# Two output instructions per image in place of four, in a convolution kernel paced by VectorE

## The reference

```python
def _gn(v, G=32, eps=1e-05):            # group norm, 4 channels a group, no affine part
    g = v.reshape(B_, G, C_ // G, H_, W_)
    m = jnp.mean(g, axis=(2, 3, 4), keepdims=True)
    s = jnp.var(g, axis=(2, 3, 4), keepdims=True)
    return ((g - m) / jnp.sqrt(s + eps)).reshape(v.shape)

wq = ternary(weight)                    # Wp, -Wn or 0 by a threshold
out = conv_general_dilated(x_, wq, (1, 1), padding=((1, 1), (1, 1)))   # 128 -> 128, 3 x 3
x = x + (out(_gn(x)) + bias[None, :, None, None])
```

## Time and profile before

| | |
|---|---|
| median of 3 runs | 581.22 us (580.83, 581.22, 588.1) |
| profiled execution | 588.38 us, span 586.6 us |
| DVE busy | 545.3 us, 93%, 508 instructions |
| PE busy | 535.1 us, 91%, 3223 matmuls |
| ACT busy | 504.4 us, 86% |
| POOL busy | 172.5 us, 29% |
| mean granted TensorE clock | 0.984 |
| moved by DMA | 153.35 MB, mean 261 GB/s |

### The profile page before, as it was taken

How to read it: one execution, slowest core, us unless ns; L and a number is a source line. 1 busy time by engine, 2 the same in 40 slices (tenths; PEclk the granted TensorE clock), 3 DMA queues, 4 the chain that set the end, 5 groups by cost and what they waited for, 6 DMA issues and landing times.

```text
span 586.6 us, 9218 instructions
## 1 busy us (share of the span) xinstructions
PE 535.1 (91%) x3223; PEld 319.1 (54%) x3223; DVE 545.3 (93%) x508; ACT 504.4 (86%) x482; POOL 172.5 (29%) x108
## 2 busy tenths in 40 slices
PE   0368999999999999999999799999999999999993
PEld 0234555555555555555565455655555555555551
DVE  2986999999999999999999879999999999999972
ACT  2478999998999999998998689999999999999840
POOL 1203222333332223333332133322233333222372
PEclk9979999999999999999999989999999999999998
DMA  7400999999999999999999998999999999999765
GB/s 289 189 0 2 287 279 284 285 276 297 296 303 272 298 282 291 283 299 290 289 289 251 269 267 264 300 289 269 285 286 281 302 296 297 292 275 270 208 152 224
DMA packets 27954, 153.35 MB, mean 261 GB/s; under 512 B 3488, under 2 KB 3488, under 8 KB 27936
## 3 DMA queue, kind: packets, MB, share of 16 engines
q1 hardware_dynamic: 19008, 103.36, 46.5%
q0 software_dynamic: 8928, 49.78, 42.0%
HBM read 51.97 MB, written 51.38 MB: 176 GB/s over the span
## 4 chain that ended last, share of the span: by engine, by line
DVE 62%; issue 23%; DMA 5%; PE 4%; POOL 2%; ACT 2%; DVEq 1%; POOLq 1%; SPq 0%; ACTq 0%
DVE parts L556 22%; DVE y L566 16%; DVE plane L514 10%; DVE plane L520 8%; PE even_rows L651 2%; DMA y<-x 2%; DMA x<-in_x_dram 2%; DVE newton L545 1%; PE odd_rows L651 1%; POOL plane L294 1%; POOL c_sb L320 1%; DVE plane L526 1%; DVEq L150 1%; DMA y<-in_L_conv_weight_dram 1%; DVE neg_var L534 1%
## 5 line engine op out<-in xcount | busy, mean ns | idle before, releaser
L651 PE MATMUL odd_rows<-parts,w_lhsT 128*128 128x385 f16 (+1 forms) x1536 | 268.9, 332 | 7.8 <-DVE parts L556 7.6
L651 PE MATMUL even_rows<-parts,w_lhsT 128*128 128x385 f16 (+1 forms) x1536 | 266.9, 331 | 9.5 <-DVE parts L556 7.0
L556 DVE SCALAR_TENSOR_TENSOR parts<-plane,norm_scale,parts 128x1568 f16<-128x1568 f32 x128 | 235.3, 1845 | 5.3 <-ACT parts L368 5.2
L294 POOL TENSOR_TENSOR plane<-x 128x1512 f32<-128x1512 f32 x32 | 109.1, 3409 | 388.1 <-DVE parts L556 379.9
L651 PEld LDWEIGHTS even_rows<-parts,w_lhsT 128*128 128x128 f16 x1536 | 149.8, 98 | 116.9 <-issue 12.6
L368 ACT ACTIVATE parts<-plane,norm_scale 128x1568 f16<-128x1568 f32 x128 | 201.2, 1597 | 11.8 <-ACT plane L389 5.3
L651 PEld LDWEIGHTS odd_rows<-parts,w_lhsT 128*128 128x128 f16 x1536 | 149.1, 100 | 109.2 <-DVE parts L556 9.6
L374 ACT ACTIVATE junk<-x 128x3136 f16<-128x3136 f32 x32 | 89.9, 2809 | 18.7 <-DMA x<-in_x_dram 18.6
L395 ACT ACTIVATE junk<-x,negmean 128x3136 f16<-128x3136 f32 x32 | 93.0, 2906 | 0.1
L566 DVE SCALAR_TENSOR_TENSOR y<-even_rows,out_scale,d_sb 128x784 f32<-128x784 f32 x64 | 63.2, 1028 | 6.3 <-POOL d_sb L320 6.3
L566 DVE SCALAR_TENSOR_TENSOR y<-odd_rows,out_scale,c_sb 128x784 f32<-128x784 f32 x64 | 63.1, 1027 | 1.6 <-PE odd_rows L651 1.6
(11 more groups left out here) (53 smaller groups left out, 107.8 us busy)
## 6 DMA issues: line engine op xcount, KB each, us to landing
x<-in_x_dram SPq DMA_DIRECT2D x64, 784.0 KB, 7.1
out_dram<-y SPq DMA_DIRECT2D x64, 784.0 KB, 5.5
y<-x POOLq DMA_DIRECT2D x62, 784.0 KB, 8.6
y<-in_L_conv_weight_dram SPq DMA_DIRECT2D x1, 576.0 KB, 3.6
bias_sb<-in_L_conv_bias_dram SPq DMA_DIRECT2D x1, 0.5 KB, 3.2
wp_sb<-in_L_conv_Wp_dram SPq DMA_DIRECT2D x1, 0.5 KB, 3.6
wn_sb<-in_L_conv_Wn_dram SPq DMA_DIRECT2D x1, 0.5 KB, 4.3
```

What stands on the lines that cost most here:

```text
L294: nc.gpsimd.tensor_tensor(plane[B][:, 0:PAIRS - 1, :], even[:, 0:PAIRS - 1, :], even[:, 1:, :], ALU.subtract).then_inc(plane_ready[B], 1)
L556: nc.vector.scalar_tensor_tensor(part(img, j, LO), plane[j][:], norm_scale[:, b_slice(img)], part(img, j, HI), ALU.mult, ALU.subtract).the ...
L651: ins = nc.tensor.matmul(product_ps(odd, b, b + 1)[:, 0, :, to:to + n], w_lhsT[:, prod, kw, :], part(img, prod, which)[:, b * BANK_ROWS:(b ...
```

## The change

For every image but the last, VectorE issues one output instruction over all four banks of the even rows, then one over those of the odd rows, 1568 columns each. Each waits for the whole product, for both halves' stores of the image two before, and adds 2 to its count when it is done. The last image keeps its four halves.

```diff
+                def output_image(img, odd):
+                    prod, other, ready, done = ((A, d_sb, d_ready, even_done), (B, c_sb, c_ready, odd_done))[odd]
+                    dve.wait_ge(product_done[prod], img.half(HALVES - 1, 1, 1))
+                    dve.wait_ge(ready, img.count(plus=1))
+                    for h in range(HALVES):
+                        wait(dve, y_stored[img.pair][h], img.pair_turns(16))
+                    y = y_sb[img.pair][:].rearrange("p (b r o) w -> p b r o w", b=BANKS, o=2)[:, :, :, odd, :]
+                    nc.vector.scalar_tensor_tensor(y, product_ps(odd), out_scale[:, p, 0:1], other[:],
+                                                   ALU.mult, ALU.add).then_inc(done, HALVES)
...
-                    if now:
+                    if now and nxt:
+                        output_image(now, EVEN)
+                        output_image(now, ODD)
+                    elif now:
                         for odd in (EVEN, ODD):
                             for h in range(HALVES):
-                                output_rows(now, h, odd, last=not nxt)
+                                output_rows(now, h, odd, last=True)
```

## The result

| | before | changed |
|---|---|---|
| median of 6 runs | 586.82 us (580.83 to 597.51) | 601.26 us (600.83 to 602.77) |
| profiled execution | 588.38 us, span 586.6 | 602.27 us, span 600.5 |
| period of a steady image | 16.62 us | 17.31 us |

The ratio is 1.0296, 95% interval 1.0253 to 1.0338: slower. It compares the fast runs alone (597.51 is left out of it, 2.9% above the fastest of its kernel), while the medians are those of all runs. The three runs of before that came with the result (597.51, 585.53, 589.23) lie above the 580.83 and 581.22 that the prediction started from; the changed kernel's six lie within 2 us.

A forecast was written before the change was run, and what follows sets the result against it. VectorE was taken to bound the kernel by its issue order. From 581.46 us, 30 periods each 0.70 longer (+ 21.0) and the last slot (+ 0.7) gave 603.2 us, +3.8%, range 599 to 609.5.

The forecast's parts named there:

- VectorE bounds, with a saving of 0.24 us per image: VectorE's issue order sets the 16.62 us period; fusing saves a fixed part of about 0.12 us per output.
- C waits for the whole even output: TensorE's next product C starts at s + 1.92 instead of s + 1.16, s being the even output's start.
- L534 and its slack of 0.07 us: VectorE's variance operation, reading a sum formed behind C, starts at s + 6.22 after idling 0.94 us.
- Period 17.32: Next even output 11.10 us after L534, so 17.32 us per steady image against 16.62: +0.70.
- the ring over two images: With L534's wait gone, the odd output's wait for all of product B gives periods of 16.5 on average.
- The covers: TensorE, ScalarE, GpSimd and DMA do not bind first; GpSimd's residual issue comes only 0.1 to 0.2 us later.
- The last slot, + 0.7: After output 30, C's late start delays ScalarE's copy and GpSimd's adds by 0.6 to 0.8 us: + 0.7.
- The kept saving (1): VectorE's 0.24 us per image come through: 574 us, or 578 with a two-image ring; decided at L534; 4%.
- the partial one (2): No measurable change, up to 592 us: ScalarE or TensorE catches up, so half the added wait disappears; 3%.
- the clock (3): TensorE's new idle of 0.9 us per image brings one slow product each, + 30 x 2.9, about 690 us; 3%.
- (4): Late loads remain as in the profiled execution and the 588.1 run: up to 610 us; 10%.
- The step that took 581.46 as the time of before: Profiled execution 588.38 less 6.92 us for three slots stretched by a late load of x: 581.46.

The follow-up runs named there:

- Experiments 1: Changed kernel with one parity fused, the other in halves: even only 602.46 us, ratio 1.0271; odd only 582.31 us, ratio 0.9965.
- experiment 2: Kernel before, nothing fused, but banks 0 and 1 of product C wait for both even halves: 607.1 us, ratio 1.0353.
- Experiment 3: Changed kernel with L534 behind the low part of A: 584.11 us; or instead with the variance matmul ahead of C's last bank: 583.04 us.
- experiments 1 to 5: Those listed here, plus controls with L534 behind A's low part: kernel before, nothing fused, 586.62 us; only odd output fused, 582.34 us.
- experiment 5: First-half loads one slot earlier, SP's list without a loop: kernel before 583.14 us; changed kernel 604.15; odd output fused with L534 moved 579.72.
- experiment 6: Changed kernel with L534 behind A's low part, earlier loads, and next image's plane A made between the two outputs: 649.37 us, ratio 1.1056.

## Why the prediction was right, step by step

- **VectorE bounds, with a saving of 0.24 us per image.** Right. Both fused outputs are 1.84 us long and 1.76 apart from what follows; with the wait away, the short one of the alternating periods is 16.37 = 16.62 - 0.25.
- **C waits for the whole even output.** Forecast s + 1.92, measured s + 1.91. Experiments 1 and 2 show that this wait is the whole loss in each period: with it alone the loss is there, without it (odd only) it isn't.
- **L534 and its slack of 0.07 us.** Forecast s + 6.22, measured s + 6.22; idle 0.94 forecast, 0.85 measured as the profile counts idle time, from the end of an instruction and not from its next start. Experiment 3 shows that this is the one path: two unlike cuts of it bring the period back.
- **Period 17.32.** Measured 17.31. The forecast of the ring over two images once this wait is gone (16.5 on average, through product B and the odd output) held too: 16.37 and 16.64 in turn. In the slot where the odd output waits for B it begins 2.02 us instead of 1.76 behind the even one, and the period that follows is the 16.64.
- **The covers.** GpSimd's residual issue came at s + 4.17, not at s + 3.6 to 3.7: it starts 0.57 us after the odd output's end, with up to 0.6 us of idle in 29 slots. I had put that latency too low. Nothing that binds stood behind it: no load came late in the loop. ScalarE's copy of C waited as said, from s + 6.1.
- **The last slot, + 0.7.** Wrong, in its sign too: the profiled execution is 1.56 us shorter behind output 30. ScalarE's copy of C did start 0.8 us later, and so did GpSimd's first add into c_sb, but counted from output 30 that add ended no later: it took 3.60 us before and 2.53 after, and ended 1.7 us behind the end of VectorE's last low part in both traces (568.07 to 569.77 before, 583.28 to 584.97 after). So VectorE's row of instructions set it, 0.25 us earlier by the fused outputs, and the last image's even output came 14.39 us behind output 30 where it was 14.65. The other 1.30 us lie behind VectorE's last instruction, from which it is 8.3 us to the end before and 6.9 after, with only the last stores left. From output 30 to the end it is 26.1 to 29.5 us among the kernels of experiments 1 to 5; I took one sample of it as fixed.
- **The time, 603.2 against 601.26.** That it is so near is in part luck. Against the profiled execution, 602.27, the forecast is 0.9 high: 2.26 too much for the last slot and 0.1 in the periods, against 1.49 that output 0 came later (54.90 for 53.41; it varies from 52.45 to 54.90 among the kernels here, and the forecast has no term for it). The median is another 1.0 below the profiled execution.
- **Rivals.** The kept saving (1) and the partial one (2) fell with the period; the clock (3) did not fall in the steady part: the granted clock is 1.00 over the 30 periods in spite of 0.71 us without a matmul in each. The wait does open one longer gap, 2.4 to 2.5 us instead of 1.56 ahead of product C of image 1; in the traces of seven kernels here that have it, that product ran at a granted clock of 1.00 in four (the changed kernel among them, 4.15 us) and took 5.82 or 5.83 us in three, with a granted clock of 0.72 from 54 to 60 us, so in part at the lower of the two levels: 1.7 us more, once an execution. (4), late loads in the changed kernel, didn't come: none of six runs is above 602.8. Its counterpart did: late loads are common before. The step that took 581.46 as the time of before described its best runs; four of the six took 4 to 16 us more. That is why a forecast of + 3.8% met a ratio of 1.030, and experiment 5, with no late loads on either side, gives 1.036. The chances of rivals 1 and 2 add up to 7%, and the times worked out for both lie within 2% of before; the prediction counts 4% there and 3% under it.

## What to carry to other kernels

A fused instruction saves its fixed part where its engine is full, and delays everyone who could start on the first half of its result: before counting the saving, follow that first half to the next thing that returns to the full engine, here a sum one column wide with 0.07 us of slack. Split what another engine waits for and fuse what nobody waits for: the even output in halves and the odd one whole, with L534 moved, was the version that gained, about 1% (ratio 0.9908, and 0.9882 with the earlier loads). And when one kernel's runs scatter over 15 us and the other's over 2, the ratio holds a second effect. Here the waits for DMA named it, and by their longest (4.4 us) more than by their sum: 26 waits of at most 1.1 us, 11.4 us in all, lengthened no period in the kernel with all periods at 16.50.

## What the runs showed of the hardware

- **VectorE beside GpSimd.** A subtraction of 128x1512 float32, both inputs in SBUF, takes 1.73 us alone (all 32 in the kernel before, 1.723 to 1.729); in experiment 6 its median is 3.41 us, and in the rows above it ends 1.6 us after GpSimd's, as if it had been held until that one ended and had then run nearly its normal time. Had both run at half speed, it would have ended 0.8 us after, and GpSimd's would not have kept its 3.41. The outputs, which read PSUM and SBUF, ran beside the same GpSimd instruction at 1.84. The Trainium skill, SBUF — State Buffer, section SBUF: two separate sides, describes the port pair that the two engines share as an exclusive lock for a whole instruction, which a VectorE operation with two SBUF inputs needs against a GpSimd one that reads SBUF. The trace agrees. The last slot shows it the other way round: GpSimd's add of 784 columns, 1.84 us alone, took 2.53 when begun at 582.44 inside a low part of VectorE that ended at 583.28. In the kernel before the PSUM outputs stand where GpSimd subtracts (153.13 to 156.99 and 153.30 to 156.70).
- **The doubled count.** A VectorE instruction that adds 2 to a semaphore released TensorE 0.07 us after its end; the second half in experiment 2, which adds 1, did so after 0.05.
- **Twice the work, not quite twice the time.** From PSUM, 784 columns are 1.03 us long and 0.94 from start to start; 1568 are 1.84 and 1.76. The fixed part that fusing saves is 0.12 us in this kernel.
